# A fused decoder layer on one core: slot writes a batch's body later, the choice of experts in two parts, next keys ahead of the last cross transposes

## The chip, the cores and the metric

The kernel runs on one core of one Trainium2 chip. The metric is the device time of one execution, in microseconds. Three runs of the kernel before took 1125.99, 1131.67 and 1133.46 us (median 1131.67). The profiled execution took 1131.91 us.

The engines are called by these names: PE (matmuls; PEld are its weight loads), DVE (vector), ACT (scalar), POOL (GpSimd) and SP (it issues DMAs). Each runs its own list of instructions in order; semaphores order them against each other.

## The reference, cut to what matters

There are 8 batches of 256 tokens, width 512, in float32. One decoder layer is computed:

```
x = x + attn(layernorm(x))            # 16 heads, 4 key/value heads, ALiBi, mask; queries scaled by
                                      #   cw = sigmoid(sum |x|)
x = x + cross(layernorm(x), ctx)      # 32 query heads, 8 key/value heads of 16; keys = values = ctx
x = x + ffn(layernorm(x))             # 32 experts, 4 per token, capacity 128, plus a shared expert

_gate:  scores = sigmoid(x @ gate_w.T);  sc = scores + gate_bias
        group_scores = sum of the top 2 of each of 4 groups of 8;  keep the 2 best groups
        topk_idx = top 4 of what is kept;  topk_w = scores[topk_idx] / sum * 2
_moe:   slot of a (token, expert) pair = how many earlier pairs chose the same expert
        buf[expert, slot] = x[token];  h = silu(buf @ w1) * (buf @ w3);  out += topk_w * (h @ w2)
shared: (silu(x @ shared_gate) * (x @ shared_up)) @ shared_down
```

## The kernel before, in words

**Bodies.** A software pipeline runs ten bodies, k = 0 to 9 (`pipelined`, L297). In body k the flags say what is done: `a` (k < 8) is the self-attention of batch k and the projections around it, `x` (1 to 8) the cross-attention of batch k-1, `g` (2 to 9) the choice of experts and the slots of batch k-2, `n` (k < 7) the first norm of batch k+1. The shared expert's work is cut into 48 pieces of 8 matmul steps of 128x256 (`shared_step`, L1133); 26 of them are spread over bodies 2 to 8 (`FIRST_PIECE`, L42), four in each of the bodies 3 to 8. After the bodies come the rest of the pieces and then the 32 experts one after the other: POOL gathers an expert's tokens by the slot table, PE, ACT and DVE compute, and POOL adds the rows to the output with an indirect DMA (L581), each waiting for the one before.

**A body on PE.** First the weights cw (L1183, tile `qa`) and the keys and values of batch k (L1192, tile `va`, two halves of 8 matmuls), then three of the four query groups (L1226). Then 32 units of cross scores (L1312, v = 0 to 31), each into one of the two banks of `qx`; DVE takes the maximum of each (L981), and PE may write unit v when the maximum of v-2 is done. Between the units stand the last query group, the transposes of values and context, steps of the shared expert (L1148, L1156), the transposes of the third norm (L1204), the gate's logits (L1215), and from v = 17 on the self scores (L1260). Then comes the second stage: 32 units of keyed cross scores (L1368) that ACT turns into exponentials (L713, copied by the helper at L592), each odd one followed by a product with the values (`xweigh`, L1379). Beside the first of them stand 8 units of keyed self scores (L1397) and the products `weigh(0)` to `weigh(3)` (L1400, four heads each), each of which waits until DVE has divided the one before out of tile `va` (`at_ready`, L1027 to L1029). Then `project(0)` and `project(1)` (L1430, tile `qa`) multiply by Wo. DVE adds the result to the tokens, takes the second norm (with POOL for the power, L473), and writes `xn2`; PE transposes it (L1123) at unit `AT_NORM`. `cross_back(0)`, `(1)` and `(2)` (L1443) transpose the cross-attention's output back, DVE divides it and adds it to the tokens (`cross_out`, L1051). The body ends with the counting matmuls of the expert choice (L1515 to L1519) and `cross_back(2)`.

**The expert choice on DVE.** `choose` (L836) is a chain of small instructions, each waiting for the one before. It stands after the last cross rows and ahead of the first division `at_ready`. `take_slots` (L878) turns the counts into slot numbers at the end of the body and waits until the slot writes before it have landed (`sc_out`).

**POOL.** In each body it adds the projection's bias to the tokens (L525, two instructions), then does the last steps of the shared expert's pieces as they end at v = 7, 15, 23 and 31 (L502, L504, L508, or L510), then the powers of the norms (L473, L479). At the end of the body stand the slot writes: a copy of token numbers (L543) and 8 indirect DMAs of 128 rows (L548). The bias add of the next body stands behind them.

**The order of shared pieces.** At a piece's first step PE waits until ACT has evicted the piece before it (`wait_evicted`, L281; the pieces use the banks `pt`, `qa`, `pt`, `va` in turn). ACT's eviction waits for POOL's last step of the piece before (`sh_h`).

```
    def cross(v):                                            # ACT, L708
        act.wait_ge(s["xst_unit"], k * XU - XU + v + 1)
        ...
        copy(ex[v % 4], xbank[v % 2], "xe_ready", ACT.Exp, scale=float(XD) ** -0.5)
    ...
    for v in range(LEAD + AU, XU):                           # ACT, L746
        cross(v)
        if n and v == 15:
            norm_apply(1, k + 1, xn1)
        if n and v == 16:
            token_sums(k + 1, 0)
            token_sums(k + 1, 1)
```

## Time and profile before

| | |
|---|---|
| profiled execution | 1131.91 us |
| its span | 1130.1 us |
| median of three runs | 1131.67 us |
| PE busy | 946.1 us (84%) |
| DVE busy | 582.9 us (52%) |
| ACT busy | 348.1 us (31%) |
| POOL busy | 255.1 us (23%) |
| granted clock of PE, mean | 0.918 of full speed |

The busy times are sums over stages with different limits, so the table alone does not say which wait ends last. A row of the timeline gives start, duration, engine, source line, instruction, output <- input and count; in square brackets stands the idle time of the engine before it and what ended that. PE's durations include the time that a result takes to leave the engine, so rows of PE overlap. The label "remote" is given to a releaser that the profile can't name.

### The profile page before, as it was taken

The numbers are of one execution on the slowest core, as the hardware profiler recorded it, in microseconds if no ns is written. First come the engines' busy times: TensorE is split into PE (matmuls) and PEld (weight loads), VectorE is DVE, ScalarE is ACT, GpSimd is POOL, SyncE is SP. The second block draws the span as 40 slices with busy tenths as digits, with TensorE's granted clock in tenths as the row PEclk, the third lists the DMA queues.
The fourth block names the chain that finished last, engine by engine and source line by source line (L and its number), as shares of the span: only waits on it lengthen the run. The fifth ranks groups of instructions, "written<-read, shape, count | busy, mean of one in ns | idle before, by whom it ended". The sixth has DMA issues, their size and how long they took to land.

```text
span 1130.1 us, 16122 instructions
## 1 busy us (share of the span) xinstructions
PE 946.1 (84%) x6123; PEld 573.7 (51%) x6168; DVE 582.9 (52%) x1300; ACT 348.1 (31%) x699; POOL 255.1 (23%) x272
## 2 busy tenths in 40 slices
PE   5376998989889789798978989878999998898990
PEld 4335545646645564574555466445477454444440
DVE  2245847857676585676668557575542122122120
ACT  4021064154145235316423622532610122121120
POOL 4001001012310510411141051032115033333332
PEclk9578599999899899989989989999999999999995
DMA  4903203202202300230230130052053199799851
GB/s 130 302 1 85 48 2 94 58 3 76 76 22 62 87 5 2 85 104 3 73 97 21 33 105 16 2 165 98 19 198 80 52 324 320 249 303 282 276 97 25
DMA packets 68640, 115.13 MB, mean 102 GB/s; under 512 B 11377, under 2 KB 39473, under 8 KB 68560
## 3 DMA queue, kind: packets, MB, share of 16 engines
q1 hardware_dynamic: 55236, 94.42, 25.9%
q0 software_dynamic: 9872, 16.54, 7.1%
q10 hardware_dynamic: 3456, 3.15, 0.9%
q8 instruction: 49, 0.80, 0.3%
q14 instruction: 27, 0.22, 0.1%
HBM read 70.90 MB, written 16.88 MB: 78 GB/s over the span
## 4 chain that ended last, share of the span: by engine, by line
PE 51%; DVE 19%; DMA 16%; issue 5%; ACT 3%; SPq 2%; another core or an unknown queue 1%; POOL 1%; POOLq 0%; DVEq 0%; ACTq 0%
DMA out<-arena,iw 15%; PE qa L1430 5%; PE qx L1312 5%; DVE mxx L981 5%; PE pt L1148 4%; PE qa L1148 4%; PE qa L1226 4%; PE vb L1379 3%; DVE rd L1027 3%; PE qx L1368 2%; ACT arena L592 2%; SPq L353 2%; PE va L1192 2%; PE qa L1260 2%; PE qa L1559 2%
## 5 line engine op out<-in xcount | busy, mean ns | idle before, releaser
L981 DVE TENSOR_REDUCE mxx<-qx 128x2 f32<-128x512 f32 x256 | 170.0, 685 | 95.1 <-PE qx L1312 68.6
L592 ACT ACTIVATE arena<-qx 128x512 f32<-128x512 f32 x256 | 145.6, 601 | 146.9 <-PE qx L1368 138.1
L1312 PE MATMUL qx<-arena 96*128 96x256 bf16 x512 | 110.8, 308 | 35.6 <-DVE mxx L981 33.7
L592 ACT ACTIVATE arena<-qa 128x512 f32<-128x512 f32 (+2 forms) x125 | 67.3, 540 | 220.2 <-PE qa L1559 99.0
L1559 PE MATMUL qa<-arena 128*128 128x512 f32 x256 | 115.9, 595 | 0.8 <-ACT arena L592 0.8
L473 POOL TENSOR_TENSOR rstd<-mv,power 128x2 f32<-128x2 f32 x24 | 16.8, 702 | 436.6 <-DVE mv L816 436.6
L1368 PE MATMUL qx<-arena 98*128 98x512 bf16 x256 | 91.3, 394 | 14.0 <-DVE mxx L981 8.3
L1312 PEld LDWEIGHTS qx<-arena 96*128 96x128 bf16 x512 | 47.8, 107 | 89.2 <-DVE mxx L981 55.6
L581 POOL DMA_INDIRECT out<-arena,iw x32 | 50.5, 1577 | 160.3 <-DMA out<-arena,iw 95.8
L1379 PE MATMUL vb<-arena 128*32 128x256 f32 x1024 | 82.8, 395 | 1.9 <-ACT arena L592 1.2
L1148 PE MATMUL pt<-arena 128*128 128x256 f32 x256 | 71.9, 394 | 3.9 <-ACT arena L592 2.3
L1559 PEld LDWEIGHTS qa<-arena 128*128 128x128 f32 x256 | 47.0, 194 | 47.1 <-issue 47.1
L1106 DVE SCALAR_TENSOR_TENSOR arena<-arena,qa 128x256 f32<-128x256 f32 x32 | 13.5, 421 | 110.9 <-ACT arena L592 106.9
L548 POOL DMA_INDIRECT slot_table<-sdat,slot_u x64 | 65.1, 1017 | 23.5 <-issue 17.1
L592 ACT ACTIVATE arena<-pt 128x512 f32<-128x512 f32 (+1 forms) x68 | 37.3, 548 | 100.8 <-PE pt L1148 35.3
L1027 DVE RECIPROCAL rd<-va 128x192 f32<-128x192 f32 x32 | 43.4, 1357 | 48.0 <-PE va L1425 47.8
L1430 PE MATMUL qa<-arena 128*128 128x512 f32 x128 | 61.6, 628 | 5.6 <-DVE arena L1029 5.6
L1546 PE MATMUL qx<-arena 128*128 128x512 f32 x128 | 63.9, 624 | 0.7 <-DVE arena L1097 0.7
L1260 PE MATMUL qa<-ks,qs 100*128 100x128 f32 x256 | 56.1, 352 | 7.3 <-issue 7.3
L1368 PEld LDWEIGHTS qx<-arena 98*128 98x128 bf16 x256 | 24.0, 98 | 69.3 <-issue 38.2
L592 ACT ACTIVATE arena<-arena 128x512 f32<-128x512 f32 (+3 forms) x40 | 25.5, 637 | 98.8 <-DVE arena L933 53.0
L1148 PE MATMUL qa<-arena 128*128 128x256 f32 x176 | 52.0, 426 | 2.2 <-issue 2.2
(193 smaller groups left out, 1546.7 us busy)
## 6 DMA issues: line engine op xcount, KB each, us to landing
arena<-in_L_ffn_w SPq DMA_DIRECT2D x96, 512.0 KB, 6.1
qs<-arena SPq DMA_DIRECT2D x24, 384.0 KB
arena<-arena SPq DMA_DIRECT2D x72, 128.0 KB, 2.4
res<-in_x SPq DMA_DIRECT2D x8, 512.0 KB, 8.2
xnd<-arena SPq DMA_DIRECT2D x8, 512.0 KB
ks<-arena SPq DMA_DIRECT2D x48, 64.0 KB
arena<-arena SPq DMA_DIRECT2D x48, 64.0 KB, 2.0
arena<-arena ACTq DMA_DIRECT2D x24, 128.0 KB, 2.8
```

The costliest lines, as they stand in the source:

```text
L548: nc.gpsimd.indirect_dma_start(slot_table, bass.IndirectOffsetOnAxis(ap=slot_u[:, c:c + 1], axis=0), sdat[:, c, :], None, bounds_check=NE ...
L592: nc.scalar.activation(dst, src, func, **kw).then_inc(s[signal], 1)
L981: v_.reduce_max(mxx[:, col:col + 3:2], xbank[v % 2].rearrange("p (h n) -> p h n", h=2), AX.X).then_inc(s["x_max"], 1)
L1027: link(v_.reciprocal(rd[:], va[:, S + GLOB:2 * S]))
L1148: op = mm(bank[:, part * S:part * S + S], w[:, c % DC, m * P:m * P + P], xt3[:, b % XRING, c % DC, :], start=c % DC == 0, stop=c % DC == D ...
L1260: op = mm(abank[1 - u % 2][:, h * P:h * P + P], qs[0:rows, q * 4 + h, blk * GLOB:blk * GLOB + P], ks[0:rows, blk, q, :], start=False, stop ...
L1312: op = mm(xbank[v % 2][:, h * S:h * S + S], qxs[0:XSPLIT_ROWS, query_at(kv * 4 + half * 2 + h), t * P:t * P + P], kxs[1 - k % 2][0:XSPLIT_ ...
L1368: mm(xbank[v % 2], kxs[1 - k % 2][0:XSPLIT_ROWS + SHIFT_ROWS, kv, t * P:t * P + P], qxs[0:XSPLIT_ROWS + SHIFT_ROWS, h:h + 3:2, :], start=T ...
L1379: op = mm(vb[at_:at_ + 32, kv % 2 * S:kv % 2 * S + S], vx[:, t, kv, :], ex[(2 * w + g4 // 2) % 4][:, g4 % 2 * S:g4 % 2 * S + S], start=t = ...
L1430: op = mm(qa[:, t * D:t * D + D], at[:, q, t * P:t * P + P], wo_s[:, q, :], start=q == 0, stop=q == DC - 1)
L1546: op = mm(xbank[0], hte[e % 2][:, c, :], h2[e % EU][:, c, :], start=c == 0, stop=c == 1)
L1559: op = mm(abank[e % 2], xgt[e % 2][:, c, :], h13[e % EU][:, :, c, :], start=c == 0, stop=c == DC - 1)
```

## The change

Five edits, all in the order of work; no instruction's shape changes.

1. POOL's slot writes of a batch move out of the end of its body. They now stand in the next body behind the piece that ends at v = 23 (`AT_SLOTS`). Body 9 does those of body 8 at its start and its own at its end.
2. `choose` is cut in two. In the bodies with self-attention, `choose_groups` stands behind the fourth division, ahead of the wait for `project(0)`, and `choose_experts` behind the first half of the residual add, ahead of the wait for `project(1)`. In bodies 8 and 9 both stay where `choose` was.
3. The cw matmuls and the first half of the key/value matmuls of batch k+1 (`keys`) move from the start of body k+1 to the end of body k, ahead of `cross_back(2)`.
4. In the second stage one unit more stands ahead of `weigh(3)` and two more ahead of the projections; the transposes of the second norm move from behind unit 23 to behind unit 25, and `cross_back(0)` and `(1)` from 19 and 25 to 20 and 26.
5. A piece of the shared expert waits for the eviction of the piece two before it, in the bodies too.

```diff
-        AT_HALF, AT_ROWS = 17, 29
+        AT_HALF, AT_ROWS, AT_SLOTS = 17, 29, 23
-        AT_OUT, AT_NORM, AT_FIRST = 19, 23, 28
+        AT_OUT, AT_NORM, AT_FIRST = 20, 25, 28
@@ POOL
-                for v in range(XU):
-                    for i in pieces_ending(k, v):
-                        shared_out(i)
-                if n:
-                    norm_scale(1, k + 2)
-                    norm_shift(1, k + 2)
-                if a:
-                    norm_scale(2, k + 1)
-                if x:
-                    norm_scale(3, k)
-                    norm_shift(3, k)
-                if g:
-
+                def tokens_to_slots(k):
                     pool.wait_ge(s["slot_ready"], k - 1)
-                    if isinstance(k, int) and k == 2:
+                    if k == 2:
                         pool.wait_ge(s["init_out"], 16)
                     nc.gpsimd.tensor_copy(sdat[:, :, 0].rearrange("p (t k) -> p t k", t=2),
                                           token[:, bass.ds(k * 2 - 4, 2)].unsqueeze(2).broadcast_to([P, 2, TOPK])
...
                         nc.gpsimd.indirect_dma_start(
                             slot_table, bass.IndirectOffsetOnAxis(ap=slot_u[:, c:c + 1], axis=0), sdat[:, c, :], None,
                             bounds_check=NE * CAP - 1, oob_is_err=False).then_inc(s["sc_out"], 16)
+
+                for v in range(XU):
+                    for i in pieces_ending(k, v):
+                        shared_out(i)
+                    if k > 2 and v == AT_SLOTS:
+                        tokens_to_slots(k - 1)
+                if n:
+                    norm_scale(1, k + 2)
+                    norm_shift(1, k + 2)
+                if a:
+                    norm_scale(2, k + 1)
+                if x:
+                    norm_scale(3, k)
+                    norm_shift(3, k)
+
+                if k == B + 1:
+                    tokens_to_slots(k)
@@ DVE
-            def choose():
+            def choose_groups():
...
                 link(v_.tensor_scalar(sel[:], sel[:], 1.5, None, ALU.is_lt))
+
+            def choose_experts():
+
                 by_group = scb[:].rearrange("p t (g e) -> p t g e", g=GRP)
...
+                def choice_free():
+                    dve.wait_ge(s["th_ready"], k - 1)
+                    hold(dve, s["pos_t"], k - 2)
...
-                    dve.wait_ge(s["th_ready"], k - 1)
-                    hold(dve, s["pos_t"], k - 2)
-                    choose()
+                if g and not a:
+                    choice_free()
+                    choose_groups()
+                    choose_experts()
...
+                    if g:
+                        choice_free()
+                        choose_groups()
                     dve.wait_ge(s["bo_added"], k + 1)
                     for t in range(2):
                         dve.wait_ge(s["wo_done"], k * 2 + t + 1)
                         link(v_.tensor_tensor(tile(k, t), tile(k, t), qa[:, t * D:t * D + D], ALU.add))
                         op = norm_tile(2, k, t)
+                        if g and t == 0:
+                            choose_experts()
@@ PE
-                    if i >= 1:
-                        wait_evicted(pe, i - 1 if i < POOLED else i - 2)
+                    if i >= 2:
+                        wait_evicted(pe, i - 2)
...
-                if a:
+                def keys(k):
...
-                    if g:
+                    if k >= 2:
                         pe.wait_ge(s["x2"], k * 3 - 4)
                     if k == 0:
                         pe.wait_ge(s["wkv_in"], 16)
-                    for half in range(2):
-                        for c in range(DC):
-                            op = mm(va[:, half * S:half * S + S], wkv_s[:, c, half * P:half * P + P], xt[:, c, :],
-                                    start=c == 0, stop=c == DC - 1)
+                    for c in range(DC):
+                        mm(va[:, 0:S], wkv_s[:, c, 0:P], xt[:, c, :], start=c == 0, stop=c == DC - 1)
+
+                if k == 0:
+                    keys(0)
+                if a:
+                    for c in range(DC):
+                        op = mm(va[:, S:2 * S], wkv_s[:, c, P:2 * P], xt[:, c, :], start=c == 0, stop=c == DC - 1)
                     op.then_inc(s["k_t"], 1)
...
                 if x:
                     cross(done)
+                    cross(done + 1)
                 if a:
                     weigh(3)
                 if x:
-                    cross(done + 1)
-                    cross(done + 2)
-                    cross(done + 3)
+                    for v in range(done + 2, done + 6):
+                        cross(v)
                 if a:
...
                     project(0)
                 if x:
-                    cross(done + 4)
+                    cross(done + 6)
                 if a:
                     project(1)
                 if x:
-                    for v in range(done + 5, XU):
+                    for v in range(done + 7, XU):
...
+                if n:
+                    keys(k + 1)
                 if x:
                     if a:
                         pe.wait_ge(s["n_rem"], k + 1)
...
                     cross_back(2)
```

## Rows read from the trace of the kernel before

**Rows 1.** The page's chain that ended last, by engine.

```profile
PE 51%; DVE 19%; DMA 16%; issue 5%; ACT 3%; SPq 2%; another core or an unknown queue 1%; POOL 1%; POOLq 0%; DVEq 0%; ACTq 0%
```

**Rows 2.** Timeline: the key/value matmuls that begin bodies 6 and 7.

```profile
556.16 3.62 PE L1192 MATMUL va<-arena 128*128 128x256 f32 x16
...
651.59 3.62 PE L1192 MATMUL va<-arena 128*128 128x256 f32 x16
```

**Rows 3.** Timeline of body 6 at its start, all engines.

```profile
561.92 1.12 POOL L548 DMA_INDIRECT slot_table<-sdat,slot_u  x1 [0.79 <-POOL sdat L543]
...
571.02 1.51 POOL L548 DMA_INDIRECT slot_table<-sdat,slot_u  x1 [0.30 <-issue]
...
572.25 0.49 ACT L592 ACTIVATE arena<-va 128x384 f32<-128x384 f32 x1 [1.17 <-remote]
...
573.88 2.08 DVE L981 TENSOR_REDUCE mxx<-qx 128x2 f32<-128x512 f32 x3 [2.19 <-remote]
...
574.63 0.61 PE L1312 MATMUL qx<-arena 96*128 96x256 bf16 x2 [2.92 <-DVE mxx L981]
```

**Rows 4.** Waits, whole run: engine, line, releaser: total us, times, longest.

```profile
DVE mxx L981 <- remote: 11.3, 5, 2.4
```

**Rows 5.** Timeline of body 2 (first row) and body 5 (the others) at their starts.

```profile
194.72 1.28 DVE L981 TENSOR_REDUCE mxx<-qx 128x2 f32<-128x512 f32 x2
...
475.03 2.52 POOL L525 TENSOR_TENSOR res<-res,bo_s 128x512 f32<-128x512 f32 x2
...
475.23 3.14 DVE L939 TENSOR_TENSOR arena<-arena 128x768 fp32r<-128x768 f32 x1
```

**Rows 6.** Stretches: PE busy (matmuls), granted clock, DMA share, GB/s; bodies 2, 6, 6.

```profile
196.80:199.80 3.00, 2.75 (x13) 0.50 1.04 211
...
580.30:583.30 3.00, 3.00 (x12) 0.50 0.00 0
583.30:586.30 3.00, 3.00 (x21) 0.95 0.00 0
```

**Rows 7.** Timeline of body 5 around the choice of experts, PE and DVE.

```profile
519.07 0.40 PE L1425 MATMUL va<-arena,ones 128*32 128x128 f32 x8
...
523.40 0.32 PE L1415 MATMUL va<-ones,arena 128*32 128x64 f32 x8 [1.89 <-DVE arena L1029]
...
513.98 0.17 DVE L838 TENSOR_SCALAR sc<-sc 128x64 f32<-128x64 f32 x1
...
517.45 0.23 DVE L855 TENSOR_TENSOR scb<-scb,sel 128x64 f32<-128x64 f32 x1
...
521.37 1.36 DVE L1027 RECIPROCAL rd<-va 128x192 f32<-128x192 f32 x1
```

**Rows 8.** Timeline of body 5 around the projections, PE, DVE and ACT.

```profile
533.54 3.70 PE L1430 MATMUL qa<-arena 128*128 128x512 f32 x8 [0.52 <-DVE arena L1029]
...
545.78 1.09 PE L1123 MATMUL pt<-ident,arena 128*128 128x128 f32 x8 [0.18 <-DVE arena L823]
...
541.69 0.69 DVE L1045 TENSOR_TENSOR res<-res,qa 128x512 f32<-128x512 f32 x1 [2.93 <-PE qa L1430]
...
532.87 1.51 ACT L598 ACTIVATE arena<-res,shift,rstd 128x512 f32<-128x512 f32 x2
```

**Rows 9.** Timeline of the end of body 5, DVE and PE.

```profile
552.97 0.48 DVE L833 TENSOR_SCALAR arena<-ident,asum 128x128 f32<-128x128 f32 x2
...
554.81 1.06 PE L1443 MATMUL pt<-ident,arena 128*128 128x128 f32 x8 [0.61 <-ACT arena L592]
```

**Rows 10.** Timeline of body 5, PE at the first step of a piece.

```profile
491.56 0.70 PE L1148 MATMUL pt<-arena 128*128 128x256 f32 x2 [0.47 <-ACT arena L592]
```

**Rows 11.** Timeline of body 8, POOL's third and fourth piece, ACT's tanh of the next.

```profile
778.71 0.72 POOL L508 TENSOR_TENSOR arena<-arena 128x256 f32<-128x256 f32 x1
...
786.10 0.85 POOL L502 TENSOR_SCALAR arena<-arena 128x256 f32<-128x256 f32 x1 [6.67 <-ACT arena L592]
...
789.15 0.38 ACT L592 ACTIVATE arena<-pt 128x256 f32<-128x256 f32 x1 [2.16 <-PE pt L1148]
```

## The prediction

> **What bounds the kernel now.** First the page's chain by engine: PE carries half of it, DVE a fifth, DMA 16%, POOL 1% [rows 1]. The DMA share is the last stage, 32 chained output scatters, which the change leaves alone; they begin when the bodies and the first experts are done, so time saved in the bodies moves them forward as a whole. What has to be read is a body. From the first key matmul of body 6 to that of body 7 are 651.59 - 556.16 = 95.4 us [rows 2]; the bodies 3 to 7 are alike. In a body PE does the work in order and stops for others at a few places. The timeline shows four that the change touches.
>
> One, at the start, beside POOL's slot writes: 9 us after the first write starts, its eighth lasts 1.51 us instead of about 1, and ACT and DVE both stop with a releaser that the profile can't name; DVE for 2.19 us, and PE for 2.92 us behind it [rows 3]. It happens five times, 11.3 us in all on DVE [rows 4], in bodies 3, 4, 6, 7 and 8. In body 2, which has no slot writes ahead of it, the same DVE instruction follows without idle time [rows 5]. In body 5 the stop is missing, but L939 takes 3.14 us there [rows 5].
>
> Two, behind this stop PE's granted clock is at 0.50: 12 matmuls in 3 us, against 21 in the next 3 us when it is back [rows 6]. In body 6 the row shown is the last of three such stretches in a row; in body 2 only one is wholly at 0.50. So 3 us at half clock lose 3 x (1 - 12/21) = 1.3 us.
>
> Three, the expert choice. PE ends `weigh(0)` at 519.47, but DVE is in the choice from 513.98 to 521.37 and divides only then; PE stands 1.89 us [rows 7].
>
> Four, the projections: PE waits 0.52 us ahead of them, and DVE idles 2.93 us ahead of the second add [rows 8]; PE waits 0.61 us for ACT ahead of `cross_back(2)` [rows 9] and 0.47 us at a piece's first step [rows 10].
>
> **The change part by part**, for a body 4 to 7.
>
> *Choice out of the first division:* -1.9 us, the idle time of rows 7. DVE divides at 519.5 and `weigh(1)` follows the unit that ends there. Late next are the divisions themselves, as now.
>
> *Order of units at the projection.* Unit 18 now stands ahead of `project(0)`. Its bank is free after exponential 16, which stands on ACT behind the first norm's apply, 1.51 us from 532.87 [rows 8]. With one unit fewer ahead of it this starts at about 532.1, so the exponential ends at about 534.2 and `project(0)` starts at 534.45 instead of 533.54: +0.9 us. `choose_groups` lies in DVE's wait of 3.7 us for `project(0)` (517.45 - 513.98 = 3.5 us, rows 7): nothing. If the groups were longer than the projection, all that follows would move with them.
>
> *`choose_experts`* takes 521.37 - 517.45 = 3.9 us [rows 7] in a hole of 2.93 us [rows 8]. The second add, the norm and `xn2` come 1.0 us later, and PE's six units ahead of the transposes fit as closely as now (0.18 us of idle, rows 8): +1.0 us.
>
> *Two units fewer behind these transposes:* about -1.0 us of PE. But DVE takes 553.45 - 546.87 = 6.6 us from their end to the diagonal [rows 8, 9], which the moved keys need: PE waits some 0.4 us there.
>
> *Keys ahead of `cross_back(2)`:* the 0.61 us wait for ACT [rows 9] is filled: -0.6 us. The matmuls only move. DVE's last `cross_out` starts about 1 us later and is covered by PE's queries. Sum of the second stage: -1.9 + 0.9 + 1.0 - 1.0 + 0.4 - 0.6 = -1.2 us.
>
> *Pieces wait two back:* three such waits a body of at most 0.47 us each [rows 10]; between 0 and 1.4 us, taken -0.7.
>
> *Slot writes away from the start.* -2.2 us for the stop [rows 3]. The clock: between nothing and 3.4 x 1.3 = 4.4 us, for 10.2 us at half clock (three stretches and a part of the next on either side); body 2, without a stop, keeps a shorter stretch [rows 6], so I take the middle, -2.2 us. The bias add then runs right behind the norm's powers, beside DVE's idle time. The copy and the 8 indirect DMAs now stand behind the piece of v = 23 and take 572.5 - 561 = 11.5 us [rows 3]. Queued behind them on POOL are the fourth piece, whose result the next body needs (nothing), and the powers of the norms, needed later (nothing). Nothing moves on SP's queue. `take_slots` waits for the writes at the body's end (nothing).
>
> *The stop at its new place.* The trace doesn't show the writes there. If the stop is theirs, it comes 9 us behind the first write, in the first third of the second stage, where ACT feeds PE. Bounds: 0 (ACT and PE have slack) and 2.2 us. I take 1.9, near the upper end, because rows 3 show it on ACT too.
>
> Sum: -1.2 - 0.7 - 2.2 - 2.2 + 1.9 = -4.4 us a body, four times -17.6. Body 3 has a shorter stretch at half clock: -3.7. Body 2, without writes or first pieces: -1.2. Body 8: its stop goes (-2.2), pieces -0.7, but here POOL's delay has a reader. The third piece ends at 779.43, the writes would end at 790; the fourth piece starts at 786.10 and ends 2.5 us later, just ahead of ACT's tanh at 789.15 [rows 11], which waits for it and has the exponentials behind it. It would end at 792.3: +3.0 us, in which the new stop is hidden. Sum +0.1. Bodies 0, 1 and 9: nothing. All: -22 us. The profiled execution took 1131.9 us, the median of the runs is 1131.7; so **1109 us**.
>
> **A rule against the trace.** In body 5 L939 starts at 475.23, while POOL's bias add runs from 475.03 to 477.55; it ends at 478.37, 0.8 us after that add [rows 5]. The Trainium skill, "SBUF — State Buffer", section "Who interferes with whom", says that a DVE instruction with two SBUF inputs and a GpSimd instruction that reads SBUF block each other for a whole instruction. Body 5 agrees. It does not explain rows 3: DVE's next instruction there reads PSUM, and ACT, which the page says never waits for a port, stops too. By the rule alone the moved bias add would save 2.2 us in body 5 and nothing elsewhere; this makes the second rival.
>
> **Rivals.**
>
> *1. The stop is hidden at its new place and the clock holds:* -1.2 - 0.7 - 2.2 - 4.4 = -8.5 us in four bodies, -7 in body 3, -1 in the rest: 1090 us. For it: DVE's load in the second stage is light once the choice is gone. Against it: body 2 falls to half clock without any stop. Chance 0.17.
>
> *2. The stop isn't the writes':* something else at the same place of each body makes it, and it stays. Then -1.2 - 0.7 a body (five times), -1.2 in body 2, +2.3 in body 8, -2.2 for body 5's port: 1132 - 9.5 - 1.2 + 2.3 - 2.2 = 1121 us. For it: no name for the releaser, and bodies so alike that any cause would keep its place. Against: body 2. Chance 0.17.
>
> *3. Slower: the stop comes with the clock.* It lands between units, PE stands 2.2 us, and the clock falls for 10.2 us as behind the old one, now where PE is nearly full, while the start keeps its half clock: -1.2 - 0.7 - 2.2 + 2.2 + 4.4 = +2.5 us in five bodies, +4.5 in body 8, -1.2 in body 2: 1148 us. It decides from 1.9/0.43 = 4.4 us at half clock on. For it: rows 3 and 6. Against: the wait of 1.89 us in rows 7 is followed by full clock. Chance 0.08; with a stretch of a third that length, 0.10, the time is about 1130.
>
> **How the numbers follow.** The forecast has 0.48. 1092 to 1124 reaches from near rival 1 over rival 2 and holds 0.8; the forecast's own range is 1102 to 1116. Within 1% (1120.4 to 1143.0) is what a measurement of this kernel can't tell from no change. Faster by more: the forecast, rival 1 and some of rival 2, 0.72. Same: the rest of rival 2 and the short stretch, 0.19. Slower: 0.09.
>
> **What would show it.** Right: no unnamed releaser in the first 20 us of a body, one about 9 us behind the first slot write in the second stage; L1415 of `weigh(1)` without idle time; `project(0)` behind a unit that waited for ACT; the second add late by 1 us behind L875; in body 8 ACT waiting 3 us for POOL's L508. Wrong: unnamed stops still behind L939 (rival 2), or three stretches at 0.50 in the second stage (rival 3).

## The result, and the profile after

The changed kernel takes 1097.9 us (median of 4 runs, 1093.6 to 1100.4) against 1129.7 for the kernel before on the same chip: ratio 0.9715, 95% interval 0.9663 to 0.9766. The forecast was 1109, its range 1092 to 1124. Sign and range hold; the sum behind the 1109 does not hold in every term, and two of its errors are large and of opposite sign, so that the total came closer than its parts.

Cut body 6 into four stages: the cross scores (first score matmul to first keyed cross unit), the second stage (to `project(0)`), the projections (to the transposes of `xn2`), and the rest (to the next body's first score matmul). Columns: stretch, its length, PE busy (matmuls), granted clock, share of the DMA engines, GB/s. The kernel before:

```profile
563.51:606.38 42.87, 35.42 (x202) 0.88 0.26 68
606.38:628.97 22.59, 19.44 (x287) 1.00 0.08 27
628.97:641.21 12.24, 11.99 (x59) 1.00 0.00 0
641.21:658.95 17.74, 16.52 (x125) 1.00 0.37 106
```

The kernel after:

```profile
542.53:575.97 33.44, 30.65 (x200) 1.00 0.34 90
575.97:599.68 23.71, 20.94 (x298) 1.00 0.08 26
599.68:612.72 13.04, 11.85 (x61) 1.00 0.00 1
612.72:629.23 16.51, 15.42 (x114) 1.00 0.37 107
```

PE's clock was 0.88 in the scores and is now 1.00; this stage alone gives 9.4 us. The second stage is 1.1 us longer, the projections 0.8 longer, the rest 1.2 shorter. Over bodies 3 to 7 the scores went from 213.8 to 166.9 us, the second stage from 115.2 to 127.8.

DVE, which [rows 4] show with an unnamed releaser, has none any more. ACT had one in the kernel before too, in bodies 4 to 8, and still has it, five times, now in the second stages of bodies 3 to 7 (waits, whole run: total us, times, longest; first before, then after):

```profile
ACT arena L592 <- remote: 12.7, 5, 5.2
...
ACT arena L597 <- remote: 11.9, 5, 3.3
```

In body 6 it stands where the prediction put it: the idle time begins 9.5 us behind the start of the first slot write and ends 11.8 us behind it. Timeline of POOL, ACT and PE in the second stage, to be held against [rows 3]:

```profile
570.81 1.09 POOL L536 DMA_INDIRECT slot_table<-sdat,slot_u  x1 [0.79 <-POOL sdat L531]
...
582.62 0.60 ACT L597 ACTIVATE arena<-qx 128x512 f32<-128x512 f32 x1 [2.28 <-remote]
...
583.28 0.39 PE L1390 MATMUL qx<-arena 98*128 98x512 bf16 x1 [1.36 <-ACT arena L597]
```

What answers to [rows 8] in body 6, at the projections:

```profile
599.45 0.39 PE L1390 MATMUL qx<-arena 98*128 98x512 bf16 x1 [0.90 <-ACT arena L597]
...
612.72 1.09 PE L1141 MATMUL pt<-ident,arena 128*128 128x128 f32 x8 [1.12 <-DVE arena L828]
...
608.45 0.17 DVE L883 SCALAR_TENSOR_TENSOR wgt<-sck,tot 128x8 f32<-128x8 f32 x1
608.65 0.69 DVE L1061 TENSOR_TENSOR res<-res,qa 128x512 f32<-128x512 f32 x1
```

The unit ahead of `project(0)` waits 0.90 us for ACT; the second add follows the last instruction of `choose_experts` without a gap. The `weigh(1)` products (L1437 here) follow without idle time, as the prediction had it. In body 8, POOL's third piece ends, the eight writes follow, and ACT waits for the fourth piece ([rows 11]: 2.16 us there):

```profile
735.37 0.72 POOL L508 TENSOR_TENSOR arena<-arena 128x256 f32<-128x256 f32 x1
...
747.05 0.88 POOL L502 TENSOR_SCALAR arena<-arena 128x256 f32<-128x256 f32 x1
...
749.62 0.38 ACT L597 ACTIVATE arena<-pt 128x256 f32<-128x256 f32 x1 [7.02 <-POOL arena L508]
```

The chain by engine, for [rows 1]: PE goes from 51 to 45%, and what it gives up is spread over the others.

```profile
PE 45%; DVE 20%; DMA 18%; issue 7%; ACT 4%; SPq 2%; POOL 2%; another core or an unknown queue 0%; POOLq 0%; DVEq 0%; ACTq 0%
```

A good mark for what the bodies take is the start of the last keyed cross unit of body 8, ahead of the last stage. Before (columns: count, duration in ns least/median/greatest, first and last start in us):

```profile
L1368 PE MATMUL qx<-arena x256: 376/389/650, 137.7 to 806.1; 98*128 98x512 bf16 x128
```

After:

```profile
L1390 PE MATMUL qx<-arena x256: 376/389/650, 138.7 to 768.5; 98*128 98x512 bf16 x128
```

That is -37.6 us, while the spans differ by 31.7. Behind the mark the kernel before took 324.0 us, the one after 329.9, 327.5 and 320.3 in three profiles, so a difference of 6 us there lies within the scatter of the last stage. Below, the mark is given beside the times.

### The profile page after: what moved, and what is told of

It reads as the page before. It is cut to its first block, busy times and chain, and to the rows that moved or that the text cites. A ratio compares the mean times of both kernels' runs of the same rounds, so it can differ in the third digit from the quotient of the medians.

```text
span 1098.4 us, 16121 instructions
## 1 busy us (share of the span) xinstructions
PE 932.3 (85%) x6123; PEld 568.8 (52%) x6168; DVE 573.2 (52%) x1300; ACT 349.3 (32%) x699; POOL 253.3 (23%) x272
## 4 chain that ended last, share of the span: by engine, by line
PE 45%; DVE 20%; DMA 18%; issue 7%; ACT 4%; SPq 2%; POOL 2%; another core or an unknown queue 0%; POOLq 0%; DVEq 0%; ACTq 0%
DMA out<-arena,iw 17%; DVE mxx L993 5%; PE qa L1248 4%; PE qx L1334 4%; PE pt L1166 4%; PE qa L1166 3%; PE qa L1452 3%; ACT arena L597 3%; PE qx L1390 3%; PE vb L1401 3%; SPq L353 2%; PE qa L1419 2%; PE qa L1282 2%; PE va L1209 2%; PE va L1215 1%
## 5 line engine op out<-in xcount | busy, mean ns | idle before, releaser
L597 ACT ACTIVATE arena<-qx 128x512 f32<-128x512 f32 x256 | 148.7, 601 | 158.9 <-PE qx L1390 133.3
L1390 PE MATMUL qx<-arena 98*128 98x512 bf16 x256 | 96.4, 400 | 33.9 <-ACT arena L597 24.6
L1334 PE MATMUL qx<-arena 96*128 96x256 bf16 x512 | 104.2, 293 | 16.3 <-DVE mxx L993 14.4
L1390 PEld LDWEIGHTS qx<-arena 98*128 98x128 bf16 x256 | 24.2, 98 | 99.1 <-ACT arena L597 55.8
L536 POOL DMA_INDIRECT slot_table<-sdat,slot_u x64 | 63.4, 991 | 23.5 <-issue 17.0
L1570 PE MATMUL qx<-arena 128*128 128x512 f32 x128 | 66.1, 642 | 0.7 <-DVE arena L1115 0.7
L1452 PE MATMUL qa<-arena 128*128 128x512 f32 x128 | 59.9, 613 | 2.0 <-DVE arena L1042 2.0
L1115 DVE TENSOR_SCALAR arena<-qx,iw 128x512 f32<-128x512 f32 x32 | 24.0, 751 | 57.3 <-PE qx L1570 50.4
```

Of the source, the lines that this page charges most:

```text
L536: nc.gpsimd.indirect_dma_start(slot_table, bass.IndirectOffsetOnAxis(ap=slot_u[:, c:c + 1], axis=0), sdat[:, c, :], None, bounds_check=NE ...
L597: nc.scalar.activation(dst, src, func, **kw).then_inc(s[signal], 1)
L1334: op = mm(xbank[v % 2][:, h * S:h * S + S], qxs[0:XSPLIT_ROWS, query_at(kv * 4 + half * 2 + h), t * P:t * P + P], kxs[1 - k % 2][0:XSPLIT_ ...
L1390: mm(xbank[v % 2], kxs[1 - k % 2][0:XSPLIT_ROWS + SHIFT_ROWS, kv, t * P:t * P + P], qxs[0:XSPLIT_ROWS + SHIFT_ROWS, h:h + 3:2, :], start=T ...
L1452: op = mm(qa[:, t * D:t * D + D], at[:, q, t * P:t * P + P], wo_s[:, q, :], start=q == 0, stop=q == DC - 1)
L1570: op = mm(xbank[0], hte[e % 2][:, c, :], h2[e % EU][:, c, :], start=c == 0, stop=c == 1)
```

## The experiments

There are twelve runs in three groups of four, each group on one chip and at one time. Ratios are to the kernel before on the same chip. No chip was used twice, so what differs between the groups may be the chip or the time; "chip" below stands for either.

### First chip: edits undone, or done alone

*Edit 1 undone*:

```
-                    if k > 2 and v == AT_SLOTS:
-                        tokens_to_slots(k - 1)
...
-                if k == B + 1:
+                if g:
                     tokens_to_slots(k)
```

> The changed kernel with edit 1 alone undone: the slot writes stand at the end of their body again. Theory (the writes bring the unnamed stop, and the half clock follows the stop): in bodies 3 to 7 DVE gets its unnamed wait of about 2.2 us back near the start of the body, three stretches of 3 us at clock 0.50 follow, and the stretch from the first cross scores to the first keyed scores grows from 33.4 to about 41 us; the second stage loses its stop (about -1.5 us a body), and body 8 loses ACT's 7 us wait for POOL. Together about +27 us: 1125 us. Rival (the score stage became shorter by the pieces' waits and the order, not by the writes): the stage stays below 35 us and the time below 1105 us.

Measured: 1073.4 us, ratio 0.9817 (0.9772 to 0.9863).

*Edit 1 alone*, on the kernel before (the writes are gone from the end of the body, as in edit 1):

```
+                    if k > 2 and v == AT_SLOTS:
+                        tokens_to_slots(k - 1)
...
+                if k == B + 1:
+                    tokens_to_slots(k)
```

> The kernel before with edit 1 alone: slot writes one body later behind the piece of v = 23. Theory: almost the whole gain of the change, since the score stage falls from 43 to about 35 us in bodies 3 to 7; the stop appears in the second stage, where DVE now also holds the choice of experts. About 1104 us. Rival (the writes matter only together with the split choice, since the stop would hit DVE inside the choice ahead of the first division): second stage +4 us a body, about 1118 us.

Measured: 1100.2 us, ratio 1.0053 (1.0025 to 1.0081): about the time that the theory gave, but no gain, since before takes 1093.3 us here. In body 8 ACT waits 6.0 us for POOL's piece, as in the kernel after.

*Edit 2 undone*: all of the choice is in DVE's earlier hole.

```
-                if g and not a:
+                if g:
                     choice_free()
                     choose_groups()
                     choose_experts()
...
-                    if g:
-                        choice_free()
-                        choose_groups()
...
-                        if g and t == 0:
-                            choose_experts()
```

> The changed kernel with edit 2 alone undone: the whole choice stands on DVE ahead of the first division again. DVE would end it about 7.4 us after the last cross rows, at 586.8 in body 6's time of the changed kernel, where the first division starts at 586.38. Theory (the stop of the slot writes halts DVE as well as ACT): the choice takes 9.5 us, the first division comes about 2.5 us later, the second add 1.0 us earlier: +1.5 us in six bodies, 1107 us. Rival (in the second stage the stop halts ACT alone, and ACT's stop delays the first product as much as the choice did): +0.4 - 1.0 us a body, 1094 us.

Measured: 1085.9 us, ratio 0.9934 (0.9909 to 0.9958). The kernel after did not run on this chip, so neither theory can be held against a time; the stages below show what the edit is worth.

*Edit 5 undone*: pieces wait one back.

```
-                    if i >= 2:
-                        wait_evicted(pe, i - 2)
+                    if i >= 1:
+                        wait_evicted(pe, i - 1 if i < POOLED else i - 2)
```

> The changed kernel with edit 5 alone undone: a piece waits for the eviction of the piece before it. Theory: 0.7 to 1.4 us a body in bodies 3 to 8, seen as idle time of PE ahead of the first step of a piece (L1166, L1174) and a score stage of about 34.4 us: 1103 us. Rival (DVE's maxima bound the score stage, so PE's waits are hidden): below 0.3 us a body, 1099 us.

Measured: 1091.6 us (1080.5 to 1094.5), ratio 0.9967 (0.9944 to 0.9989). The profiled execution is the one of 1080.5, the shortest of eleven; the ten others took 1086.8 to 1094.5, and what they had more isn't on record.

**What follows.** The surprise is the kernel before itself: 1093.3 us on this chip. None of the four profiles, wherever the slot writes stand, has an unnamed releaser on DVE or ACT. So these profiles price the other edits without the stop. (Before itself was not profiled here.) Body 6 of the kernel with edit 5 undone, the first three of the four stages:

```profile
534.97:570.25 35.28, 31.10 (x201) 1.00 0.32 86
570.25:592.13 21.88, 20.57 (x297) 1.00 0.09 28
592.13:605.17 13.04, 11.85 (x60) 1.00 0.00 1
```

With edit 2 undone, where body 6 is one of the two dearest (bodies 3 and 6):

```profile
534.10:567.54 33.44, 30.65 (x201) 1.00 0.35 90
567.54:593.57 26.03, 21.95 (x297) 0.93 0.07 24
593.57:605.70 12.13, 11.85 (x60) 1.00 0.00 1
```

First rows: the scores take 35.28 us with the pieces one back and 33.44 with two back. Edit 5 is worth 1.8 us in this body: PE's waits of 0.85 and 0.80 us at a piece's first step, in the former, are gone in the latter. Over bodies 3 to 7 the scores take 176.7 us in the former and 166.9 in the latter, so it is 9.8 us, 2.0 a body. Second rows: 21.88 us is the second stage without a stop. With the choice back it is 26.03, because PE waits for the division behind the choice, because one DVE instruction of the choice lasts 1.63 us instead of the 0.17 that it takes in the kernel after, and because the clock falls to 0.93:

```profile
572.11 1.63 DVE L849 TENSOR_TENSOR gs<-m 128x8 f32<-128x8 f32 x1
...
572.41 1.29 POOL L510 TENSOR_TENSOR res<-res,arena 128x512 f32<-128x512 f32 x1
...
580.95 0.32 PE L1432 MATMUL va<-ones,arena 128*32 128x64 f32 x8 [2.86 <-DVE arena L1042]
```

L849 ends 0.04 us behind POOL's add; in the kernel with edit 1 alone it is the same (1.64 us). Both kernels have one more such pair in body 3 (L853, 1.85 us), and none in bodies 4, 5 and 7, where POOL has other work at that moment. Delayed writes push POOL's L510 onto the choice in these two bodies, so edit 1 alone costs there, and the two edits belong together. The Trainium skill, "SBUF — State Buffer", section "Who interferes with whom", says that such a pair blocks each other for a whole instruction; here the trace agrees, in that DVE goes on when POOL's add ends. Third rows: `choose_experts` between the adds costs 13.04 - 12.13 = 0.9 us. In bodies 4, 5 and 7 the second stage with the choice back is only 1.2 us longer than without (23.46, 23.48 and 22.41 us), so there edit 2 is worth 1.2 - 0.9 = 0.3 us.

In the kernel with edit 1 undone the theory failed: there was no stop to bring back. It is the fastest of the four, but it alone has all of the edits 2 to 5, so that is no proof for the writes' old place. By the stages, the old place costs 173.6 - 166.9 = 6.7 us in the scores of bodies 3 to 7 and nothing in the second stages (109.4 us, as with edit 5 undone), and saves 29.7 - 24.2 = 5.5 us in the second stage of body 8: about nothing in all.

### Second chip: the same two kernels again, and fewer writes

> The kernel before, unchanged. In the first four experiments its time was 1093.3 us, not 1131, and no kernel there showed a stop with an unnamed releaser. Theory A: the stop is the whole difference between the two times of this kernel; this profile shows no unnamed stop, its score stages (first score matmul to first keyed cross unit) take about 33 us instead of 40.5 to 44 in bodies 3 to 7, and the time is about 1093. Rival: the stop is still there and something else is quicker (the projections, the last stage); the score stages stay at 40 or more.

Measured: 1119.0 us (1112.8 to 1123.8), DVE's unnamed stop 4 times, 9.0 us; in the bodies where it is missing on DVE, ACT has it. Score stages of 38.5 to 41.7 us in bodies 3 to 7. So this chip has the stop, and whether a kernel before of 1093 us has none could not be seen here.

> The changed kernel, unchanged, beside the kernel before on the same chip. If the gain of the first comparison (-32 us) came from the stop and the clock behind it, and before has no stop here, what is left is what the second stage gives: the first experiments put edit 1 alone at +6 us against before, and all but edit 1 at -20, so the sum is about -10 to -14 us: 1080 to 1084. Rival: after is slower than before by the stop that it shows at its new place: 1095 to 1100.

Measured: 1093.3 us, ratio 0.9751 (0.9688 to 0.9815), with five stops of 12.6 us on ACT. The expectation took a chip without the stop; what came repeats the first result.

*Half of the writes*: `for c in range(TOPK)` in place of `range(2 * TOPK)`, and the counts waited for accordingly.

> After with four of the eight slot writes of each batch (half of the token slots are left out). If the slot writes cost something where they now stand (a stop 9 us behind the first one, or the time they hold POOL), half of them cost less than half: against after -6 to -10 us, and in body 8 ACT's wait of 7 us for POOL's piece shrinks by 4.9 us. Rival: the writes at this place cost nothing beyond body 8: -4 to -5 us.

Measured: 1055.3 us, ratio 0.9410 (0.9350 to 0.9471); the mark at 744.9 us against 764.4 of after on the same chip. The rest is the last stage, 307.1 us against 327.5, which has half of the slots. No unnamed releaser on any engine, and second stages of 21.2 to 22.2 us in bodies 3 to 7: the stop goes with the second half of the writes. ACT's wait of 7 us for POOL in body 8 is gone too. -19.5 us at the mark is more than either theory said.

*Body 8's writes behind its last piece*: `v == (XU - 1 if k == B else AT_SLOTS)`.

> After with the slot writes of body 8 moved behind its last piece (v = 31 instead of 23), all else the same. Theory: in body 8 ACT's tanh waits 7 us for POOL's fourth piece, which stands behind the writes; without that wait ACT goes on 5 us earlier and so does the kernel: -4 to -5 us against after. Rival: what follows (the first experts) waits for something else, the slots among them: -1 to +3.

Measured: 1096.0 us, ratio 0.9754 (0.9691 to 0.9816): no gain. ACT's wait of 7 us for POOL is gone, but the writes now run to 757 us, inside ACT's exponentials, and the stop comes in their midst (ACT, body 8):

```profile
752.68 0.60 ACT L597 ACTIVATE arena<-vb 128x512 f32<-128x512 f32 x1 [2.34 <-remote]
754.10 0.60 ACT L597 ACTIVATE arena<-qx 128x512 f32<-128x512 f32 x1 [0.82 <-remote]
...
758.46 1.09 ACT L597 ACTIVATE arena<-qx 128x512 f32<-128x512 f32 x2 [2.37 <-remote]
```

One wait was turned into three, together 5.5 us. The time lies in the rival's range, for another reason than it gave.

### Third chip: after, its first edit undone, and a split

> The changed kernel, unchanged, so that it stands beside the three others of this call on one chip. Theory: the stop is a matter of the chip too (five times in this kernel where before took 1119 and 1131 us, and not seen in four kernels where before took 1093). Where before takes 1115 us or more, this one shows about five unnamed releasers on ACT and takes 1090 to 1098; where before takes about 1093, it shows none and takes 1079 to 1086. Rival: the stop and the time of before have nothing to do with one another; then any pairing can come.

Measured: 1091.9 us beside 1119.7 for before, ratio 0.9762 (0.9718 to 0.9806); five stops, 13.4 us. Time of before and presence of the stop go together on all three chips, as the theory had it.

> After with edit 1 undone (slot writes at the end of the body, ahead of the next bias add), beside after itself. Theory: where the stop exists, it is back at the start of the score stage on DVE, with half clock behind it, and edit 1's share of the gain is lost: 1110 to 1117, score stages of 38 us or more. Where it doesn't exist, edit 1 costs: this kernel is 6 to 12 us faster than after, 1070 to 1076. Rival: edit 1 brings nothing even where the stop exists, and the gain is edits 2 to 5: this kernel equals after within 3 us.

Measured: 1091.3 us, ratio 0.9742 (0.9699 to 0.9786), the same as after: the rival holds. The mark is at 765.8 us, that of after at 767.8. Body 6, scores and second stage:

```profile
540.64:577.19 36.55, 31.05 (x203) 1.00 0.32 83
577.19:599.08 21.89, 20.57 (x302) 1.00 0.08 28
```

The same program on the first chip, without the stop, had 34.30 us in the first row. What differs is ACT at the start of the body, here:

```profile
552.44 0.38 ACT L641 ACTIVATE arena<-pt 128x256 f32<-128x256 f32 x1 [4.56 <-remote]
```

and on the chip without it:

```profile
542.07 0.38 ACT L641 ACTIVATE arena<-pt 128x256 f32<-128x256 f32 x1 [1.14 <-PE pt L1164]
```

So the stop is there, on ACT in bodies 4 to 8; an unnamed releaser on DVE comes in only 2 of them. DVE is held in body 6 all the same, under another name. PE's score matmuls of one unit end at 549.24 us, and the maximum that needs them starts 1.1 us later:

```profile
548.85 0.39 PE L1332 MATMUL qx<-arena 96*128 96x256 bf16 x2
...
550.34 0.69 DVE L991 TENSOR_REDUCE mxx<-qx 128x2 f32<-128x512 f32 x1 [1.55 <-PE qx L1332]
```

The next maximum is 1.0 us late in the same way; PE stands 1.41 and 1.32 us for the two. The clock of this stage is 1.00 to 0.91 in bodies 3 to 7, where before had 0.92 to 0.88 in the first comparison and 0.96 to 0.91 on the second chip. Summed over these bodies, the scores take 186.7 us with the writes at the start and 166.9 with them in the second stage; the second stages take 109.4 and 127.5. Edit 1 moves 18 to 20 us from one stage to the other: 1.7 us gained in these bodies. From body 8's first score matmul to the mark it loses 5.3 us (59.9 against 54.6), where ACT waits 7.1 us for POOL.

*The eight writes in two lots of four*, behind the pieces of v = 15 and v = 23; all slots are written. The second argument says which lot, columns 0 to 3 or 4 to 7:

```
-                    if k > 2 and v == AT_SLOTS:
-                        tokens_to_slots(k - 1)
+                    if k > 2 and v in (15, 23):
+                        tokens_to_slots(k - 1, int(v == 23))
```

> After with the eight slot writes of a batch in two lots of four, behind the pieces of v = 15 and v = 23 (all slots are written). Theory: half the writes gave a kernel without any stop, so the stop belongs to eight in a row, not to a write; two lots of four with some 3 us between them give none, and in body 8 ACT waits 5 us less for POOL's last piece. Against after -8 to -14 us where the stop exists, -4 to -6 where not. Rival: what counts is how many writes are under way or done, not that they follow one another: the stop comes behind the second lot, and only body 8 gains, 0 to -5.

Measured: 1072.4 us, ratio 0.9568 (0.9524 to 0.9611), 19.5 us less than after. The mark:

```profile
L1396 PE MATMUL qx<-arena x256: 376/389/650, 138.4 to 744.3; 98*128 98x512 bf16 x128
```

That is -23.5 us against 767.8 of after on this chip. Body 6:

```profile
530.41:564.61 34.20, 31.03 (x203) 1.00 0.34 88
564.61:586.50 21.89, 20.57 (x302) 1.00 0.08 28
586.50:599.53 13.03, 11.85 (x60) 1.00 0.00 1
599.53:616.04 16.51, 15.42 (x114) 1.00 0.37 107
```

None of the second stages holds a stop, and ACT never waits for POOL's L508. The theory holds there, and the gain is larger than its 8 to 14 us: the second stages of bodies 3 to 7 are 18.1 us shorter, and body 8 up to the mark 8.3.

The scores are not quite free of it. Behind the first lot of four, which starts at 549.32 us in body 6, ACT and DVE both go on at 555.2, though the matmuls that the maximum needs had ended at 554.04. The last row is DVE's maximum at the same place in the kernel after, on the same chip:

```profile
553.66 0.38 PE L1340 MATMUL qx<-arena 96*128 96x256 bf16 x2
...
555.20 0.22 ACT L603 ACTIVATE sc<-vb 128x64 f32<-128x64 f32 x1 [9.35 <-remote]
...
555.25 0.69 DVE L999 TENSOR_REDUCE mxx<-qx 128x2 f32<-128x512 f32 x1 [2.08 <-PE qx L1340]
...
564.50 0.69 DVE L993 TENSOR_REDUCE mxx<-qx 128x2 f32<-128x512 f32 x1 [0.91 <-PE qx L1334]
```

ACT's idle time at this place is 7.5 to 7.8 us in bodies 3, 4, 5 and 7. DVE has the same in bodies 4 and 5 (1.87 and 1.82 us), and again in the next kernel. So a shorter stop of about 1 us is left behind four writes; the scores of bodies 4 to 6 are 0.5 to 0.8 us longer than in the kernel after, those of bodies 3 and 7 are within 0.1 us. Behind the second lot nothing shows.

*The split, `choose_groups` back in the earlier hole, `choose_experts` at the wait for the first projection, one cross unit fewer ahead of `project(0)`*:

```
-                if g and not a:
+                if g:
                     choice_free()
                     choose_groups()
+                if g and not a:
                     choose_experts()
...
                     if g:
-                        choice_free()
-                        choose_groups()
+                        choose_experts()
...
-                        if g and t == 0:
-                            choose_experts()
...
-                    for v in range(done + 2, done + 6):
+                    for v in range(done + 2, done + 5):
...
                     project(0)
                 if x:
+                    cross(done + 5)
                     cross(done + 6)
```

> The same, with choose_groups back in DVE's earlier hole (where all of the choice was before), choose_experts at the wait for the first projection, and one cross unit fewer ahead of project(0). Theory: the second add no longer waits for choose_experts (+1.0 us a body in the forecast) and project(0) no longer waits for exponential 16 (+0.9): against the split alone -1 to -1.9 us a body, -5 to -9 in all. Rival: DVE's earlier hole isn't free now (the divisions come later, as before), +0.5 us a body: 0 to +3.

Measured: 1062.7 us, ratio 0.9471 (0.9419 to 0.9522), 9.7 less than the split alone, the mark 8.1 less; body 6:

```profile
522.53:556.70 34.17, 31.02 (x203) 1.00 0.33 88
556.70:577.53 20.83, 20.36 (x301) 1.00 0.08 30
577.53:589.99 12.46, 12.17 (x61) 1.00 0.00 1
589.99:606.50 16.51, 15.42 (x114) 1.00 0.37 107
```

The second stage is 1.06 us shorter, the projections 0.57. This is the fastest version that writes all slots, 29.2 us below after by the medians on this chip. The theory held; the gain is at its upper end by the mark and 0.7 us beyond it by the medians.

## Why the prediction held, and where it didn't

*Bounds and places.* PE in the bodies set the time, and the stop came 9 us behind the first write at its new place: shown by the traces and, for the cause, by half the writes, by the split and by the stop that followed body 8's writes to a third place. The prediction read body 5 of the kernel before as free of the stop. It was not: ACT has an unnamed releaser there too, and DVE is late twice under PE's name (the matmuls had ended at 470.25 and 473.63). The count of five times was that of DVE alone. Before, body 5:

```profile
471.00 0.69 DVE L981 TENSOR_REDUCE mxx<-qx 128x2 f32<-128x512 f32 x1 [2.64 <-PE qx L1312]
...
474.62 0.69 DVE L981 TENSOR_REDUCE mxx<-qx 128x2 f32<-128x512 f32 x1 [1.44 <-PE qx L1312]
...
476.74 0.49 ACT L592 ACTIVATE arena<-va 128x384 f32<-128x384 f32 x1 [1.90 <-remote]
```

*Second stage and projections.* Forecast -1.2 us a body for the choice, the order, the experts, the units moved and the keys. Without a stop (split, body 6 against before): 21.89 - 22.59 = -0.7, 13.03 - 12.24 = +0.8, 16.51 - 17.74 = -1.2; sum -1.1. The sum holds; it compares two chips, as after without a stop was never profiled. Two terms can be seen by themselves: `project(0)` waits 0.90 us for ACT (+0.9 forecast) and the experts cost 0.9 us (+1.0 forecast). Both are costs, and both could be avoided in large part, as the last kernel shows: the old early hole is wide enough for the groups though not for the whole choice.

*Pieces two back.* Forecast -0.7; measured -1.8 in body 6 and -2.0 a body over bodies 3 to 7. I had bounded each wait by the single row of 0.47 us [rows 10]; PE's waits in the kernel with the edit undone are 0.85 and 0.80 us. The term failed by taking one row as the largest of its kind.

*Stop and clock at the start.* Forecast -2.2 - 2.2 = -4.4 us a body. The scores of body 6 fell by 9.4 us, of which 1.8 is edit 5: -7.6. Over bodies 3 to 7 the fall is 46.9 - 9.8 = 37.1, or 7.4 a body. The clock went from 0.88 to 1.00 over the whole stage. The mis-sized step is the middle taken for the clock, "body 2, without a stop, keeps a shorter stretch": bodies 3 to 7 keep none. At 0.88, (1 - 0.88) x 42.87 = 5.1 us of full clock were missing, more than even the upper bound of 4.4. With 2.2 to 2.9 us for the stop that makes 7.3 to 8.0. That half clock needs a stop isn't shown: body 2 of the kernel after, behind no slot writes, has 0.85 over its scores of 34.4 us.

*Stop at the new place.* Forecast +1.9 of at most 2.2. In body 6 it is 23.71 - 21.89 = +1.8, just as forecast; over bodies 3 to 7 it is 127.8 - 109.4 = 18.4, or 3.7 a body. In bodies 5 and 7 ACT is stopped for 3.3 us, and in the second stages of all but body 6 the clock falls behind the stop, most in body 4 of the kernel after (22.2 us long without a stop):

```profile
396.64:423.91 27.27, 23.64 (x298) 0.87 0.02 4
```

So rival 3's mechanism was real in part: the upper bound of 2.2 left out what the clock adds. Beside -7.4 at the old place it could not turn the sum. The two mis-sized terms, 3 us too small at the old place and 1.8 too small at the new one, partly cancelled, and that is luck: no reading of the rows made them do so.

*Body 8.* Forecast +0.1: measured -7.3 in the scores (stop, clock and pieces) and +6.8 in the second stage (24.3 to 31.1 us), where I had +3.0. ACT's wait is 7.02 us against 2.16, 4.9 more, and the clock fell behind it. The sum of -0.5 is near the forecast only because the two errors cancel.

*Rivals.* Rival 1 had the full clock right and the hidden stop wrong. Rival 2 is out: the stop moved with the writes, and in the second stages it went with half of them. Its port clash exists, at another place and pair (L849 beside L510).

**What was read right and means less than I thought.** I told the gain as that of edit 1: -2.5 of -4.4 us a body. On a chip with the stop, edit 1 undone gives the same time (1091.3 against 1091.9): what it gains in bodies 3 to 7 it loses in body 8. The gain of 28 us there is that of edits 2 to 5. Only before on the second chip has a profile to hold it against; over bodies 3 to 7 that gives 23.9 us: edit 5 (9.8 us), the second stage (116.7 - 109.4 = 7.3), what follows it (1.7), and what is left of the fall in the scores (201.6 - 186.7 - 9.8 = 5.1), a milder stop at the start. Why the stop is milder there after the other edits is not settled. In body 6 of before both ACT and DVE stop, PE stands 2.92 us at once [rows 3] and half clock follows; with edits 2 to 5 DVE is late twice, PE stands 1.41 and 1.32 us, and the clock stays at 1.00. Edit 1 alone, or another single edit, was not tried on a chip with the stop.

Left open too: what the stop is. Behind eight writes nearly all the unnamed ones end 10 to 12 us after the start of the first, on ACT, DVE or both; with body 8's writes moved behind its last piece one ends 5.7 us after it already (752.68 - 746.96). Behind four writes at v = 15 a shorter one ends 5.7 to 5.9 us after the first, and behind four at v = 23 there is none. So fewer writes in a row make the stop shorter or end it, but a number below which there is none is not shown. Of the three chips of these runs two have it, and on the third none of the four profiles has it. The same program (edit 1 undone) took 1091.3 us with it and 1073.4 without. The first comparison agrees with the former kind. Why before took 1129.7 us there and 1119 to 1120 on two other chips that have the stop isn't known; its score stages of bodies 4 to 7 were 2.2 to 4.4 us longer, and 0.88 in clock where the second chip had 0.91 to 0.96.

## What to carry to other kernels

Look for a stall in late starts too, where a row names a releaser that had long ended, and not only in rows without a name. When a burst of indirect DMAs stalls the other engines, ask first whether the burst must be one: two lots of four, with a little of POOL's own work between them, brought 19.5 us where moving all eight to another stage brought nothing net. Price a stall with the clock behind it, and look how much of the stage was at the lower level, not at one stretch. And undo each edit in the final kernel before crediting it: the edit with the clearest story here was worth nothing net, and one with a forecast of 0.7 us a body was worth 2.0.

## What was not expected of the hardware

- The same program shows the unnamed stops on one chip and none on another (or at another time, as no chip was used twice): 1091.3 against 1073.4 us for one kernel. Before took 1119 to 1130 us against 1093.3.
- Four slot writes of 1 us each in a row leave no trace on the other engines at v = 23, and about 1 us at v = 15; with eight in a row, ACT idles up to 3.3 us in the second stages, and DVE about 2.2 us in the scores of the kernel before.
- ACT and DVE can start 1.0 to 1.2 us behind the end of the matmul that they wait for (550.34 against 549.24, 555.25 against 554.04), beside slot writes.
- The granted clock of the scores fell to 0.88 behind a PE wait of 2.92 us, and stayed at 1.00 in body 6 where PE stood 1.41 and then 1.32 us.
- The granted clock fell to 0.85 over the scores of body 2 in the kernel after, with no slot writes ahead.
- A DVE instruction of 0.17 us lasted 1.63 us beside POOL's add of 1.29 us.
